# A graph network layer stack on one core: exponentials moved behind a group's evictions, and another order at the end of attention

## What is computed

```python
for i in range(4):
    y = _cond_layer_norm(x, cond, s1_w[i], s1_b[i], b1_w[i], b1_b[i])
    y = _sparse_attention(y, src, dst, wq[i], bq[i], wk[i], bk[i], wv[i], bv[i], wo[i], bo[i])
    x = x + y
    y = _cond_layer_norm(x, cond, s2_w[i], s2_b[i], b2_w[i], b2_b[i])
    y = relu(y @ m_w1[i] + m_b1[i]) @ m_w2[i] + m_b2[i]
    x = x + y
# in _sparse_attention, 4 heads of 128:
scores = einsum('ehd,ehd->eh', q[src], k[dst])
ex = exp(scores - segment_max(scores, src)[src])
attn = ex / segment_sum(ex, src)[src]
out = segment_sum(attn[:, :, None] * v[dst], src)
```

## Time and profile before

| | |
|---|---|
| median of 3 runs | 2031.95 us (2030.65 to 2033.86) |
| profiled execution | 2027.8 us, span 2026.0 us |
| mean granted TensorE clock | 0.984 |
| busy: TensorE, VectorE, ScalarE, POOL | 1789.0 (88%), 1324.8 (65%), 899.6 (44%), 392.0 us (19%) |
| chain that ended last | TensorE 61%, issue 15%, VectorE 14%, ACT 6% |
| DMA | 165.81 MB, mean 82 GB/s |

### The profile page before, as it was taken

One profiled execution on the slowest core, in us unless ns is written; L12 is line 12 of the kernel. 1 busy time (PEld: TensorE's weight loads), 2 busy tenths in 40 slices (PEclk: granted clock), 3 DMA queues, 4 the chain that ended last, 5 costly groups with the idle time before them and its releaser, 6 DMA issues.

```text
span 2026.0 us, 33390 instructions
## 1 busy us (share of the span) xinstructions
PE 1789.0 (88%) x11835; PEld 1520.1 (75%) x11835; DVE 1324.8 (65%) x2383; ACT 899.6 (44%) x1461; POOL 392.0 (19%) x469
## 2 busy tenths in 40 slices
PE   1566459999999999999999999999999999999898
PEld 0455338888878788888787888887878888878777
DVE  8899955576685555766855557668565576685744
ACT  2798534454454244544542445445323454453221
POOL 5322223000024230000242300002523000023301
PEclk9999879999999999999999999999999999999999
DMA  1300352242231022422310224223102242232122
GB/s 23 109 0 0 127 213 74 80 142 87 85 121 48 17 70 83 141 89 83 122 48 17 66 86 135 95 82 118 52 15 75 81 131 90 91 115 83 39 67 74
DMA packets 62759, 165.81 MB, mean 82 GB/s; under 512 B 5777, under 2 KB 23986, under 8 KB 62605
## 3 DMA queue, kind: packets, MB, share of 16 engines
q10 hardware_dynamic: 23040, 102.41, 15.2%
q1 hardware_dynamic: 39572, 61.45, 9.5%
HBM read 146.58 MB, written 17.02 MB: 81 GB/s over the span
## 4 chain that ended last, share of the span: by engine, by line
PE 61%; issue 15%; DVE 14%; ACT 6%; DVEq 2%; DMA 1%; ACTq 1%; POOL 0%; POOLq 0%
PE ps L1306 55%; PE ps L1488 4%; DVE PT_lo L1094 3%; ACT PT_hi L702 3%; ACT prob L691 2%; DVE prob L1078 2%; PE ps L1408 2%; DVEq L939 1%; DVE CW L950 1%; DVE x L1108 1%; DVE CW L953 1%; DVE onehot L911 1%; DVE CW L997 1%; PE ps L1679 0%; DVE cpart L900 0%
## 5 line engine op out<-in xcount | busy, mean ns | idle before, releaser
L1094 DVE TENSOR_TENSOR PT_lo<-ps,PT_hi 128x512 fp32r<-128x512 f32 x400 | 271.0, 688 | 33.0 <-ACT PT_hi L702 16.2
L691 ACT ACTIVATE prob<-prob,nmax 128x1250 f32<-128x1250 f32 x160 | 214.1, 1338 | 175.6 <-DVE nmax L1078 175.6
L702 ACT ACTIVATE PT_hi<-ps 128x512 fp32r<-128x512 f32 x400 | 231.1, 590 | 70.9 <-PE ps L1488 70.9
L1488 PE MATMUL ps<-ident,prob 128*128 128x128 f32 x1600 | 244.0, 275 | 14.3 <-DVE PT_lo L1094 13.5
L1078 DVE CUSTOM_DVE_ANT_0 prob<-ps,Lr 128x1250 f32<-128x1250 f32 x160 | 232.5, 1453 | 34.5 <-PE ps L1306 31.7
L1306 PE MATMUL ps<-PT_hi,v_hi 128*128 128x256 f32 x800 | 232.9, 291 | 20.2 <-DVE PT_lo L1094 20.2
L1488 PEld LDWEIGHTS ps<-ident,prob 128*128 128x128 f32 x1600 | 184.1, 140 | 67.8 <-DVE PT_lo L1094 47.5
L1306 PE MATMUL ps<-PT_hi,v_lo 128*128 128x256 f32 x800 | 225.8, 282 | 0.0
L1306 PE MATMUL ps<-PT_lo,v_hi 128*128 128x256 f32 x800 | 225.8, 282 | 0.0
L1306 PE MATMUL ps<-k_hi,q_hi 128*128 128x512 f32 (+2 forms) x480 | 191.6, 399 | 0.5
L1306 PEld LDWEIGHTS ps<-PT_hi,v_hi 128*128 128x128 f32 x800 | 152.4, 190 | 33.4 <-DVE PT_lo L1094 33.4
(11 more groups left out here) (209 smaller groups left out, 4106.9 us busy)
## 6 DMA issues: line engine op xcount, KB each, us to landing
Lr<-l_table ACTq DMA_DIRECT2D x160, 625.0 KB, 3.8
piece<-in_L_gnn_m_w_dram SPq DMA_DIRECT2D x32, 256.0 KB, 2.6
w_table<-CW SPq DMA_DIRECT2D x1, 6250.0 KB, 17.7
l_table<-CW SPq DMA_DIRECT2D x10, 625.0 KB, 7.0
prob<-w_table SPq DMA_DIRECT2D x10, 625.0 KB, 4.0
x<-in_x_dram SPq DMA_DIRECT2D x2, 2304.0 KB
piece<-in_L_gnn_wv_dram SPq DMA_DIRECT2D x16, 256.0 KB, 3.0
piece<-in_L_gnn_wq_dram SPq DMA_DIRECT2D x16, 256.0 KB, 4.3
```

Source lines behind the costliest of these rows:

```text
L691: act.activation(buf, buf, ACT.Exp, bias=nmax[:, i % 4:i % 4 + 1], scale=-1.0, accum_out=rsum[:, i % 4:i % 4 + 1]).then_inc(S["exped"], 1)
L702: act.activation(o, i, ACT.Copy).then_inc(S["pt_hi"], 1)
L1094: dve.tensor_tensor(lo, i, hi.bitcast(F32), ALU.subtract).then_inc(S["pt_split"], 1)
L1488: m = pe.transpose(bank(5 + n % 2, at * P, (at + 1) * P), prob[:, (NT * h + 2 * g + j) % 3, d * P:(d + 1) * P], ident[:])
```

## The change

Three things, on TensorE, ScalarE, VectorE and POOL.

1. *Groups.* ScalarE runs `exp(i)` after all five copies of a group instead of after the third, and `exp(i - 1)` ahead of `o_hi_` of the group before instead of behind it. VectorE takes both reciprocals at the start of the next group, ahead of `o_lo_`.
2. *The end of attention.* Head 3's last group has an order of its own (`close`): the product of group 3 goes over tiles 0 to 9 in order, in three parts, each ahead of a round of transposes and counted by the new semaphore `o_part`, so that the copies of rounds 0, 1 and 2 wait for the part that they overwrite. The last four projections go to banks 2, 3, 4 and 7 (`wo_bank`) in place of bank 7 for all; two come after the fifth round, one after `hidden(0, 0)`, one ahead of `hidden(1, 0)`. VectorE's adds, centers, norms and statistics of these tiles move behind the group accordingly, a weight piece (MLP2 - 1) moves behind the copy of y tile 10, and POOL's reciprocal roots of tiles 16 to 19 behind the splits of h.
3. *Start of a layer.* Jobs take banks 4 and 7 in turn, starting with 4; v0 waits for one add less of the layer before. v7 then lies in bank 4, v8 follows qk4 in bank 7, and the scores of tile 1 wait for v7's split.

```diff
-            return 7 if name in LATE_VALUES else (7, 4)[JOBS.index(name) % 2]
+            return 7 if name in LATE_VALUES else (4, 7)[JOBS.index(name) % 2]
+        def wo_bank(h, t):
+            return {NT - 4: 2, NT - 3: 3, NT - 2: 4}.get(t, 7) if h == H - 1 else 7
             if h == H - 1 and g == GROUPS - 1:
-                return {0: [MLP1], 1: [MLP1 + 1], 3: [MLP1 + 2], 4: [MLP1 + 3]}.get(r, [])
+                return {0: [MLP1], 1: [MLP1 + 1], 3: [MLP1 + 2]}.get(r, [])
...
POOL
-                        if h == H - 1 and g:
+                        if h == H - 1 and 0 < g < GROUPS - 1:
                             rsqrt(NT + 2 * g - 2)
                             rsqrt(NT + 2 * g - 1)
+                rest(MLP2 - 1)
                 for n in range(2):
                     rest(MLP2 + n)
-                rsqrt(2 * NT - 2)
-                rsqrt(2 * NT - 1)
                 for c in range(GROUPS):
                     h_rest(c, 0)
                     h_rest(c, 1)
+                    if c < 2:
+                        rsqrt(2 * NT - 4 + 2 * c)
+                        rsqrt(2 * NT - 3 + 2 * c)
...
ScalarE
-                    if r == 0:
+                    if h == H - 1 and g == GROUPS - 1:
+                        if r < 2:
+                            wait("o_part", r + 1)
+                        elif r == 2:
+                            wait("o_ready", GROUPS * h + g)
+                    elif r == 0:
                         wait("o_ready", GROUPS * h + g)
...
                         if g:
-                            o_hi_(h, g - 1)
                             exp(i - 1)
+                            if more or not last:
+                                o_hi_(h, g - 1)
                         for r in range(5):
                             pt_hi_(h, g, r)
+                            if last and not more and r == 2:
+                                o_hi_(h, g - 1)
...
-                            if r == 2 and not last:
-                                exp(i)
                             for n in pieces(h, g, r):
                                 piece_hi(n)
+                        if not last:
+                            exp(i)
...
                 y_hi_(NT)
+                piece_hi(MLP2 - 1)
                 y_hi_(NT + 1)
...
VectorE
                         if g:
-                            o_lo_(h, g - 1)
+                            recip(i - 2)
                             recip(i - 1)
+                            if more or not last:
+                                o_lo_(h, g - 1)
...
                             if last and not more:
-                                if r in (0, 3):
-                                    center(NT + r // 3)
-                                if r in (1, 4):
-                                    norm(NT + r // 3)
+                                if r == 0:
+                                    center(NT)
+                                if r == 1:
+                                    norm(NT)
+                                if r == 2:
+                                    o_lo_(h, g - 1)
...
-                            if r in (0, 2):
+                            if r in (0, 2) and not (last and not more):
...
-                            if r == 2 and not last:
-                                recip(i)
...
-                        if g and not more:
+                        if g and not last and not more:
                             stats(NT + 2 * g - 2)
                             stats(NT + 2 * g - 1)
...
+                add_wo(H - 1, NT - 4)
+                center(NT + 1)
+                norm(NT + 1)
                 y_lo_(NT)
+                add_wo(H - 1, NT - 3)
                 y_lo_(NT + 1)
+                center(NT + 2)
                 o_lo_(H - 1, GROUPS - 1)
-                center(NT + 2)
                 norm(NT + 2)
-                add_wo(H - 1, NT - 2)
-                add_wo(H - 1, NT - 1)
-                for t in (NT - 2, NT - 1):
-                    stats(NT + t)
                 for c in range(GROUPS):
                     if c < GROUPS - 1:
                         for n in (NT + 2 * c + 2, NT + 2 * c + 3):
+                            if n == NT + 2:
+                                add_wo(H - 1, NT - 2)
...
+                        if c == 0:
+                            add_wo(H - 1, NT - 1)
+                        if c < 2:
+                            stats(2 * NT - 4 + 2 * c)
+                            stats(2 * NT - 3 + 2 * c)
...
TensorE
-                        wait("x_mlp", 0)
+                        wait("x_mlp", JOBS.index(name) - 1)
...
+                def close():
+                    h, g = H - 1, GROUPS - 1
+                    for r in range(5):
+                        if r < 3:
+                            out_heads(h, g - 1, (range(4), range(4, 8), range(8, NT))[r], range(NT))
+                        turn(h, g, r)
+                        if r in (0, 3):
+                            cond(NT + r // 3)
+                    project(h, g - 1, 0)
+                    project(h, g - 1, 1)
+                    turn_y(NT)
+                    out_heads(h, g, FIRST)
+                    turn_y(NT + 1)
+                    out_heads(h, g, SECOND)
+                    hidden(0, 0)
+                    project(h, g, 0)
+                    turn_y(NT + 2)
+                    hidden(0, 1)
+                    turn_y(NT + 3)
+                    project(h, g, 1)
...
                 values(8)
+                wait("v_split", int(JOBS[-1][1]) + 1)
                 scores_a(0, 1, 0)
...
-                turn_y(NT)
-                out_heads(H - 1, GROUPS - 1, (0,))
-                turn_y(NT + 1)
-                out_heads(H - 1, GROUPS - 1, (1,))
-                project(H - 1, GROUPS - 1, 0)
-                project(H - 1, GROUPS - 1, 1)
-                for c in range(GROUPS):
+                for c in range(1, GROUPS):
                     hidden(c, 0)
```

52 lines of the change are left out of this document (30 added, 22 removed).

## The result

The change makes the kernel faster: median 1974.52 us (1972.64 to 1975.19, 4 runs) against 2032.51 us (2030.65 to 2033.86, 4 runs) for the kernel before, ratio 0.9714 (95% interval 0.9697 to 0.9731). That is 58 us less. The profiled execution took 1975.0 us (span 1973.2, granted clock 0.982); the one of before 2027.8 (span 2026.0, clock 0.984).

The account below looks back on a forecast made before the run. TensorE, busy 88%, bounds the kernel, so only removing its waits pays. Groups 28.2, layer ends 18 and starts 1.0 make 47.2 us off the profiled 2027.8: 1980.6, plus 4 for the median, 1984.5; range 1975 to 1999.

Parts of the forecast that it names:

- 60 x 0.47: In the groups: 60 waits of TensorE for round 3's PT_lo vanish, 0.47 us each, 28.2 us in all.
- (a): Layer's end: group 3's product begins with tile 0, which wants round 3 at once; new wait of 0.4 us.
- upper bound of 35: In the groups: 60 x 0.59 us saved, if the next 0.1 us of each wait go too.
- (b): Layer's end: the first conditioning matmuls wait for the last mask; new wait of 0.3 us.
- (c): Layer's end: round 3's transposes wait for round 1's difference, behind VectorE's statistics and reciprocals; 0.9 us.
- (e): Layer's end: y tile 11's transposes wait for VectorE's round 4 chain, its copy behind a weight piece's copy; 0.6 us.
- (f): Layer's end: the second pair's hidden tiles wait for y tile 13, one projection now inside that wait; 1.5 us.
- (d): Layer's end: conditioning 11 waits for normalised tile 10, and round 4's transposes for round 2; 0.4 us together.
- Rival 1: Layer's end gains little, VectorE becoming the bound there: 1.5 us a layer, 1996.5 us; chance 0.14.
- Rival 4: Granted clock at layer ends: shorter waits remove the last layer's fall, 1983; or falls at each end, 1989, chance 0.08.
- Rivals 2, 3 and 5: New oT_lo wait in groups, 1998.5, chance 0.07; late moved exponential, 2062, 0.03; something else holding round 3, 2013, 0.03.

Follow-up runs that it names:

- exp_last_only: Kernel before with only `exp(i)` moved behind the five copies of a group; 1994.61 us, ratio 0.9812.
- swap_only: Kernel before with only `exp(i - 1)` put ahead of `o_hi_` and `recip(i - 1)` ahead of `o_lo_`; 2029.74 us, ratio 0.9985.
- group_only: Kernel before with only part 1 of the change, the groups' new order; 1991.68 us, ratio 0.9808.
- end_only: Changed kernel with parts 1 and 3 undone, so only the new end of attention; 2011.34 us, ratio 0.99.
- one_bank: Changed kernel with all four last projections back in bank 7; 2000.88 us, ratio 0.9838.
- shift4: Changed kernel with 4 long-fulfilled waits on TensorE's queue ahead of the loop over the layers; 1973.24 us, one run.
- shift64: Changed kernel with 64 long-fulfilled waits on TensorE's queue ahead of the loop over the layers; 1966.34 us, one run.
- before_again: Kernel before, unedited, run once more for a second profile; 2033.26 us, one run.

## Why the prediction was right or wrong, point by point

- **What bounds it, and the cause of the group's wait: right.** `exp_last_only` and `swap_only` show that the one exponential ahead of round 3's copy made the wait. Everything that was moved stayed in time, oT_lo with the 0.7 us that the sum gave it.
- **The price of the wait: wrong, too small.** The step that failed is "60 x 0.47": "I take 0.47, the start-to-start figure". The start-to-start figure was read up to the matmul that waited and not to the one behind it. That one comes 0.22 us later instead of 0.12, by the weight load that the wait uncovers, and with it the wait costs 0.57 (period 11.55 to 10.99, forecast 11.08). 60 x 0.57 = 34, as `exp_last_only` and `group_only` show (34.2); the table has 32.4 since the new wait (a) of 0.4 us a layer lies ahead of the product's start. That is 5.8 us that the forecast lacked. Its upper bound of 35 ("if the next 0.1 go too") covered it. But the range was built without that bound: "down by the upper bounds of the end (6) and of the starts and the clock (3 to 4)" leaves out the 7 us by which the groups could give more, and 1984.5 less all three is 1968.
- **The layer's end: right, 18 forecast and 17.9 found.** Past the product's start the ends save 4.98, 4.88 and 4.78 us in layers 1 to 3 and 6.35 in layer 4; the wait (a) takes 0.4 of each. Without the clock's part of 1.5 in layer 4 that is 17.9, 4.5 a layer, as taken. Its terms, in layer 2 from start to start: (a) 0.37 for 0.4; (b) 0.22 for 0.3; (c) 0.77 for 0.9; (e) 1.2 for 0.6; (f) 1.55 for 1.5; (d) does not show. Sum 4.1, as laid out, though by luck: (e) took what (d) left. In (e) VectorE's chain ended when laid out, 13.0 us behind the product's start, but TensorE stood there after 11.8 us and not after 12.5. Rival 1 (the end gains little) fell: `end_only` has the short ends too. Without the new banks it would have been worse than before (`one_bank`).
- **The clock: a rival's case.** Rival 4's first half, "if shorter waits remove this, 1983", came true: layer 4's end now runs at 1.00 and gives 1.5 us. That was put beside the sum and not in it.
- **Banks of the start: right in kind.** 1.0 in layer 4 (measured 0.98), 0 at the loop backs, by the pause that `shift4` and `shift64` place in the code. But the starts and the rest cost 3.1 us against the 2.5 that the wraps save, so the part shows as a loss of 0.6 us where 1.0 was entered. Of that 1.1 us is layer 1's start, where the clock rises later in the profiled execution of after (window 284 to 290: 0.85, before 1.00).
- **From the profiled execution to the median: wrong.** Profiled, the sum gave 1980.6 and 1975.0 came: 5.6 us short, the groups' 5.8 and the clock's 1.5 less the starts' 1.6 and the end's 0.1. The other 4.4 us of the 10 are this step: "the runs' median is 2031.95, 4 us above that execution, so 1984.5". The 4 us above are mostly no constant of the measurement but falls of the clock in the layers' ends, which `before_again` has and the profiled one had not, but for layer 4's. This is read from one execution near the median (2033.26), on another chip, and not from many. The change took the falls of the ends away; its own median lies 0.5 us below its profiled execution. With this term and the right price of the wait the forecast would have been about 1975.
- **Rivals 2, 3 and 5** fell by the list of waits: no wait for oT_lo or prob in the groups, and round 3 was held by nothing else. So did rival 4's second half: no layer end after the change shows a granted clock of 0.50.

The parts nearly add up: `group_only` saves 40 us and `end_only` 20 at the median, the whole change 58.

## What to carry to other kernels

Read the cost of a wait from the last start ahead of it to the second start behind it, and compare with the undisturbed spacing: here the idle column said 0.31, the first start 0.47, and the wait cost 0.57, sixty times over. A sum made on one profiled execution needs that execution's clock beside the median's: where the runs spread with their mean clock, waits of some microseconds close together also cost a fall now and then, and taking them away pays that too. And a pause for "issue" just behind a loop back, with no semaphore to account for it, can be a matter of where code lies; shifting the code ahead of the loop is a cheap experiment.

## What was not expected of the hardware

- After a wait of TensorE on a semaphore, the waiting fp32 matmul of 256 columns holds the next for 0.22 us instead of 0.12 (760.36 and 760.58 above), in all 64 waits of the kernel before: its weight load starts with it (760.36) and not 0.11 us ahead of it.
- 5 to 8 us of idle time spread in pieces of up to 2.1 us over a layer's end of 31 us bring falls of the granted clock to 0.50 in some executions and not in others; two waits of 2.4 and 2.1 us within 7 us brought a fall of about 10 us in `one_bank`. What decides between executions stays open.
- 64 fulfilled waits ahead of the loop cost nothing that shows and take away two pauses of about 2 us with the clock falls behind them, about 7 us in all. In the kernel before they bring as much (7.7 us by the ratio, 6.7 in the two starts), although the layer ends of that execution showed more falls of the clock (33.4, 35.0 and 32.6 us in layers 2 to 4); it was the slowest of ten, 2029.46 against a median of 2025.94. Whether the shift has a part in those falls was not tried.
